# Attention on one core: softmax denominators from added key tiles, and a new order of masks, ropes, statistics, roots and denominators

## The reference

```python
q = (X @ Wq)...; k = (X @ Wk)...; v = (X @ Wv)...    # 16 query heads, 8 key/value heads, 32 wide
q = q * cos + _rotate_half(q) * sin                  # rope; k the same
k = jnp.repeat(k, n_rep, axis=1)                     # one key head serves two query heads
att = jnp.einsum('bhqd,bhkd->bhqk', q, k) * scale
att = SOFTCAP * jnp.tanh(att / SOFTCAP)              # cap at 50
att = jnp.where(causal[None, None], att, -jnp.inf)
att = jax.nn.softmax(att, axis=-1)
y = jnp.einsum('bhqk,bhkd->bhqd', att, v)
return y @ Wo
x = x + _L0_attn_ref(_layernorm(x, axis=-1), ...)
```

## Time and profile before

| | |
|---|---|
| median of 3 runs | 1013.99 us (1012.54 to 1015.94) |
| profiled execution | 1013.01 us, its span 1011.3 us, mean granted clock 0.977 |
| attention stage | about 346 to 684 us of the span, first scores at 365.7 us |
| busy over the whole span | PE 933.9 us (92%), DVE 654.7 (65%), ACT 537.3 (53%), POOL 484.2 (48%) |

### The profile page before, as it was taken

The page is one execution under the profiler, slowest core; times in us unless marked ns, Lnnn a source line. Parts: engine busy times, 40 slices in busy tenths (PEclk is TensorE's granted clock), DMA queues, the critical chain, the costliest instruction groups (busy, mean ns, idle before and its releaser), DMA issues. The chain is left out here.

```text
span 1011.3 us, 18264 instructions
## 1 busy us (share of the span) xinstructions
PE 933.9 (92%) x6274; PEld 695.2 (69%) x6274; DVE 654.7 (65%) x1670; ACT 537.3 (53%) x798; POOL 484.2 (48%) x534
## 2 busy tenths in 40 slices
PE   2999998999999589999999999868999989999998
PEld 1788885777778465666666666546888767777787
DVE  4888767544444456877877877646888676453435
ACT  3766642132233258888888888836667622232322
POOL 5333203555642067687687687524413124555540
PEclk9999999999999789999999999987999999999999
DMA  5434225777884300101101000103332256777735
GB/s 189 119 92 134 67 81 160 168 180 177 188 190 105 125 1 12 32 21 31 31 21 31 31 21 29 56 19 90 111 106 74 71 175 143 180 170 187 178 60 172
DMA packets 95432, 101.90 MB, mean 101 GB/s; under 512 B 18688, under 2 KB 86656, under 8 KB 95360
## 3 DMA queue, kind: packets, MB, share of 16 engines
q1 hardware_dynamic: 83072, 83.17, 27.6%
q0 software_dynamic: 12288, 17.83, 10.6%
HBM read 65.44 MB, written 35.54 MB: 100 GB/s over the span
## 5 line engine op out<-in xcount | busy, mean ns | idle before, releaser
L80 PE MATMUL gu<-x_hi,gu_hi 128*128 128x512 f32 x308 | 140.3, 455 | 4.7 <-DVE act_gu L1124 4.7
L82 PE MATMUL gu<-x_lo,gu_hi 128*128 128x512 f32 x308 | 122.8, 399 | 0.0
L81 PE MATMUL gu<-x_hi,gu_lo 128*128 128x512 f32 x308 | 122.4, 398 | 0.0
L1627 POOL TENSOR_SCALAR_AFFINE_SELECT probs_at<-probs_at 128x1024 f32<-128x1024 f32 x64 | 77.4, 1209 | 81.6 <-ACT probs_at L1551 80.9
L1543 ACT ACTIVATE capped_at<-scores_at 128x2048 f32<-128x2048 f32 x64 | 93.2, 1457 | 29.9 <-PE scores_at L1447 29.9
L671 POOL DMA_INDIRECT rows<-z_rows,slots x64 | 67.7, 1058 | 75.7 <-DVE slots L1115 56.7
L957 ACT CAST a_hi<-act_gu 128x512 fp32r<-128x512 f32 x96 | 59.2, 616 | 84.3 <-DVE act_gu L1124 66.9
L1551 ACT ACTIVATE probs_at<-capped_at 128x2048 f32<-128x2048 f32 x64 | 95.2, 1487 | 2.0
L80 PE MATMUL down<-down_hi,a_hi 128*128 128x256 f32 x300 | 93.8, 313 | 0.2 <-DVE a_lo L1134 0.2
L1005 ACT ACTIVATE y<-gu,rows 128x256 f32<-128x256 f32 x64 | 30.4, 474 | 109.8 <-PE gu L887 93.2
L867 PE MATMUL zT<-w_gu,xT 128*128 128x352 f32 x256 | 86.3, 460 | 0.0
(11 more groups left out here) (228 smaller groups left out, 2547.6 us busy)
## 6 DMA issues: line engine op xcount, KB each, us to landing
w_gu<-in_w_gate SPq DMA_DIRECT2D x64, 176.0 KB
w_gu<-in_w_up SPq DMA_DIRECT2D x64, 176.0 KB
w_down<-in_w_down SPq DMA_DIRECT2D x64, 176.0 KB
z_rows<-z SPq DMA_DIRECT2D x16, 512.0 KB, 3.1
acc<-base SPq DMA_DIRECT2D x10, 512.0 KB, 3.5
out<-base SPq DMA_DIRECT2D x10, 512.0 KB, 3.6
x_f<-in_X SPq DMA_DIRECT2D x8, 512.0 KB, 4.6
xn_at<-acc SPq DMA_DIRECT2D x16, 256.0 KB, 2.7
```

The costliest lines, as they stand in the source:

```text
L80: nc.tensor.matmul(out, w_hi, x_hi, start=first, stop=False)
L81: nc.tensor.matmul(out, w_lo, x_hi, start=False, stop=False)
L82: return nc.tensor.matmul(out, w_hi, x_lo, start=False, stop=last)
L1627: pool.affine_select(out=diag, in_=diag, compare_op=ALU.is_ge, fill=zero, base=0, pattern=[[0, JH], [0, REP], [1, P]], channel_multiplier= ...
```

## The change

The products with ones no longer run with the values of each unit. For the first 128 queries only key tile 0 counts; for the last 128 both tiles do. VectorE now adds the two tiles' probabilities for those last 128 queries (`add_tiles`, into a new buffer `both`), and a new TensorE step, `denominators`, makes eight products of 256 columns per group: four with ones and the first 128 queries of tile 0, four with ones and `both`. `probs` has one buffer for each of the four units, and `exponential` waits on the `denominators` of the slot before in place of the values of two units back. `invert` waits on `denominators`.

The lists change too. TensorE: `denominators`(b-1, 1) stands behind the first two pieces of the projection, `denominators`(b, 0) behind the output. ScalarE: `y_hi_part`(b, 0) moves from the end of the slot into the next slot, behind `take_values`(b, 1). GpSimd: root first, and the fourth mask ahead of the third rope. VectorE: `statistics` first, `y_lo`(b-1, 0) and `invert`(b-1, 1) behind the first two `turn`, `aT_lo_part` ahead of `divide`(b, 0), and the two `add_tiles`. Input buffers: 6 in place of 4. The waits at the end of the stage and ScalarE's loop (unrolled by 6 in place of 4) follow from that.

```diff
-        HELD = 4
+        HELD = 6
...
-        probs = sb("probs", [P, 2, JH, W], F32)
+        probs = sb("probs", [P, UNITS, JH, W], F32)
+        both = sb("both", [P, GROUPS, JH, REP, P], F32)
...
 (weighted_values, TensorE)
-                    at_least(pe, den_taken, b * GROUPS + g)
                 n = REP * (SEQ - t * P)
-                for bank, ones in ((den, True), (pv, False)):
+                for j in range(JH):
+                    w = v[:, q, t, (JH * g + j) * HD:(JH * g + j + 1) * HD]
+                    out = pv[j * HD:(j + 1) * HD, :].rearrange("p (r s) -> p r s", r=REP)[:, :, t * P:SEQ]
+                    last = nc.tensor.matmul(out, w, probs[:, u, j, 0:n].rearrange("p (r s) -> p r s", r=REP),
+                                            start=t == 0, stop=t == QT - 1)
+                last.then_inc(pv_done, 1)
+
+            def denominators(b, g):
+
+                pe.wait_ge(summed, b * GROUPS + g + 1)
+                at_least(pe, den_taken, b * GROUPS + g)
+                for of_both in (False, True):
                     for j in range(JH):
-                        w = m.ones_f[:] if ones else v[:, q, t, (JH * g + j) * HD:(JH * g + j + 1) * HD]
-                        out = bank[j * HD:(j + 1) * HD, :].rearrange("p (r s) -> p r s", r=REP)[:, :, t * P:SEQ]
-                        last = nc.tensor.matmul(out, w, probs[:, u % 2, j, 0:n].rearrange("p (r s) -> p r s", r=REP),
-                                                start=t == 0, stop=t == QT - 1)
-                last.then_inc(pv_done, 1)
+                        if of_both:
+                            weights = both[:, g, j]
+                        else:
+                            weights = probs[:, QT * g, j].rearrange("p (r s) -> p r s", r=REP)[:, :, 0:P]
+                        at = slice(of_both * P, (of_both + 1) * P)
+                        out = den[j * HD:(j + 1) * HD, :].rearrange("p (r s) -> p r s", r=REP)[:, :, at]
+                        last = nc.tensor.matmul(out, m.ones_f[:], weights, start=True, stop=True)
+                last.then_inc(den_done, 1)
...
 (slot_of, TensorE)
                     project(b + 1, 1 - q, 1)
+                if behind:
+                    denominators(b - 1, 1)
                 score_unit(b, q, 1)
...
                     output(b - 1)
+                denominators(b, 0)
                 weighted_values(b, q, 2)
...
 (exponential, ScalarE)
-                at_least(act, pv_done, b * UNITS + max(u - 1, 0))
+                at_least(act, den_done, (b - 1) * GROUPS + u // QT + 1)
...
 (slot_of, ScalarE)
                     take_values(b - 1, 1)
+                    y_hi_part(b - 1, 0)
...
-                y_hi_part(b, 0)
-                if further:
                     aT_hi_part(b + 2)
...
 (slot_of, GpSimd)
+                if further:
+                    root(b + 2)
                 causal(b, 0)
...
-                if further:
-                    root(b + 2)
                 causal(b, 2)
+                causal(b, 3)
                 if ahead:
                     rope(b + 1, 1 - q, 2)
-                causal(b, 3)
...
 (VectorE)
+            def add_tiles(b, g):
+
+                dve.wait_ge(probs_ready, b * UNITS + QT * (g + 1))
+                at_least(dve, den_done, (b - 1) * GROUPS + g + 1)
+                first = probs[:, QT * g].rearrange("p j (r s) -> p j r s", r=REP)[:, :, :, P:SEQ]
+                second = probs[:, QT * g + 1, :, 0:REP * P].rearrange("p j (r s) -> p j r s", r=REP)
+                dve.tensor_tensor(both[:, g], first, second, ALU.add).then_inc(summed, 1)
...
 (slot_of, VectorE)
-                if behind:
-                    y_lo_part(b - 1, 0)
-                    invert(b - 1, 1)
+                if further:
+                    statistics(b + 2)
                 if ahead:
                     turn(b + 1, 0)
                     turn(b + 1, 1)
                 if behind:
+                    y_lo_part(b - 1, 0)
+                    invert(b - 1, 1)
                     divide(b - 1, 1)
-                if further:
-                    statistics(b + 2)
                 if ahead:
                     turn(b + 1, 2)
                 if behind:
                     y_lo_part(b - 1, 1)
-                invert(b, 0)
+                add_tiles(b, 0)
                 if behind:
                     residual(b - 1)
-                divide(b, 0)
+                invert(b, 0)
                 if further:
                     aT_lo_part(b + 2)
+                divide(b, 0)
+                add_tiles(b, 1)
```

More of the change, by code:

```diff
@@ L1362, in attention @@
         pv_done = sem("pv_done")
+        summed = sem("summed")
+        den_done = sem("den_done")
         taken = sem("taken")
@@ L1394, in _ @@
                 if b == SEQS - 2:
-                    for n in range(HELD):
+                    for n in range(2 * BLK // SEQ):
                         sp.wait_ge(stored[n], 16)
@@ L1403, in _ @@
             for n in range(HELD):
-                sp.wait_ge(stored[n], 16 * (SEQS // HELD))
+                sp.wait_ge(stored[n], 16 * len(range(n, SEQS, HELD)))
         @block.tensor
@@ L1516, in _ @@
             weighted_values(SEQS - 1, 1, 3)
+            denominators(SEQS - 1, 1)
             output(SEQS - 1)
@@ L1548, in exponential @@
                 act.wait_ge(capped_ready, b * UNITS + u + 1)
-                at_least(act, pv_done, b * UNITS + max(u - 1, 0))
+                at_least(act, den_done, (b - 1) * GROUPS + u // QT + 1)
                 n = REP * (SEQ - u % QT * P)
-                nc.scalar.activation(probs[:, u % 2, :, 0:n], capped[:, u % 2, :, 0:n], ACT.Exp,
+                nc.scalar.activation(probs[:, u, :, 0:n], capped[:, u % 2, :, 0:n], ACT.Exp,
                                      scale=SOFTCAP).then_inc(exp_ready, 1)
@@ L1600, in _ @@
             take_values(SEQS - 1, 1)
+            y_hi_part(SEQS - 1, 0)
             y_hi_part(SEQS - 1, 1)
@@ L1625, in causal @@
                 n = REP * (SEQ - u % QT * P)
-                diag = probs[:, u % 2, :, 0:n].rearrange("p j (r s) -> p j r s", r=REP)[:, :, :, 0:P]
+                diag = probs[:, u, :, 0:n].rearrange("p j (r s) -> p j r s", r=REP)[:, :, :, 0:P]
                 pool.affine_select(out=diag, in_=diag, compare_op=ALU.is_ge, fill=zero, base=0,
@@ L1686, in turn @@
                 dve.stream_shuffle(turned[:, n], bank[:], [(i + HD // 2) % HD for i in range(HD)]).then_inc(turned_ready, 1)
+            def add_tiles(b, g):
[4 more added lines that the diff above has]
+                dve.tensor_tensor(both[:, g], first, second, ALU.add).then_inc(summed, 1)
             def invert(b, g):
                 n = b * GROUPS + g
-                dve.wait_ge(pv_done, b * UNITS + QT * (g + 1))
+                dve.wait_ge(den_done, n + 1)
                 dve.transpose(den_T[:].rearrange("p n d -> p (n d)"), den[:]).then_inc(den_taken, 1)
```

## The result

The changed kernel takes 1034.2 us (median of 6 runs, 1033.02 to 1035.26) against 1014.4 before: ratio 1.0195, 95% interval 1.0182 to 1.0209, so 2% slower. Its profiled execution spans 1033.5 us against 1011.3. The starts of the transposes and of the last residual divide the 22.2 us between them. Between the transposes of sequences 2 and 15 it is 266.7 in place of 248.3 (+18.4); from the first transposes to those of sequence 2, 29.6 in place of 30.5 (-0.9); from those of sequence 15 to the last residual, 53.1 in place of 48.7 (+4.4); all the rest is +0.3.

The account below looks back on a forecast made before the run. TensorE bound the kernel before; after the change the loop through VectorE and ScalarE would, at 20.7 us a slot. 13 periods (+20.5), slot 0 (-1.3) and the end (+1.7) gave 1033.9 profiled, 1034.5 forecast; range 1017 to 1046.

Parts of the forecast that it names:

- the ring: Attention slot: loop from one slot's transposes through VectorE and ScalarE to the next slot's, forecast to set a 20.7 us period.
- TensorE's gain: Attention slot: denominators at 0.46 us a set, 1.84 in place of 2.70, so TensorE's work falls 0.86 to 18.26 us.
- Steps 1 to 10: Attention slot: walk from transposes through VectorE, GpSimd and ScalarE to the next transposes, cap2 at 12.86, end at 20.70 us.
- The reading of how VectorE and GpSimd hold each other: Two-input VectorE operations and GpSimd's: whichever starts first finishes, the other runs afterwards; `divide` ended 0.55 us after GpSimd.
- `add_tiles` at 1.22: VectorE's 128x1024 add of two SBUF operands: forecast at its lower bound of 1.22 us, a sign of being right.
- the bound of 2.7: VectorE's `add_tiles`: upper bound of 2.7 us if it runs behind a 1.60 us GpSimd instruction.
- step 4: VectorE's statistics, moved to the slot's front: 1.18 us to the last instruction plus 0.17 for it, ready at 5.35.
- Step 6, the race: First group's `y_lo` on VectorE starts 0.11 us after GpSimd's rope multiply, waits it out and ends at 9.56.
- rival A: `y_lo` starts before GpSimd's rope multiply and takes 0.68 us: period 19.95, +11.2, 1024.5 us; chance 0.22.
- Rival C, the clock: TensorE's clock halves after its idle time ahead of the last scores in every slot: period 22.3, 1055 us; chance 0.08.
- The sum: Whole kernel: 13 periods x 1.58 = 20.5 us, slot 0 -1.3, the end +1.7, together +20.9.
- Rival B: TensorE stays the bound in the attention slots and the time falls by 10.8 to 1002.5 us; chance 0.08.

Follow-up runs that it names:

- e2: Changed kernel with the second group's add cut from 1024 columns to 2 for all sequences but the first: 1015.5 us.
- e4: Changed kernel with `y_lo` of the first group moved behind the second group's division: 1015.0 us.
- e3: Changed kernel with the first group's add cut from 1024 columns to 2 for all sequences but the first: 1034.6 us.
- e5: Changed kernel with the first group's `y_lo` behind the second division and the statistics computed one sequence further ahead: 1008.7 us.
- e1: Changed kernel with the statistics back behind the previous group's division and GpSimd's root behind the second rope: 1030.1 us.
- e10: Changed kernel with GpSimd's loop over pairs of slots written out, same instructions: 1035.2 us.
- e7: Changed kernel with sixteen more product instructions per slot on TensorE, in its idle time ahead of the last scores: 1028.2 us.

## Why the prediction was right

The forecast was 1034.5, the measurement 1034.2, and the mechanism is the one forecast: cutting a piece of the ring speeds the kernel up (e2, e4), cutting as much VectorE time beside it does not (e3). By the steps:

- *TensorE's gain.* The new products take 0.46 us a set as forecast (533.96 to 534.42 in the timeline), so the work went, and e5 shows what it is worth when TensorE is near to binding: 0.47 of the 0.86 us a slot.
- *Steps 1 to 10.* In the slot shown above cap2 starts at 13.06 after the transposes (forecast 12.86), the next transposes at 20.88 (20.70). The 0.20 us of idle time that only this slot has make up the difference; the others of its kind have cap2 at 12.5 to 12.8 and the next transposes at 20.4 to 20.6, a little under the forecast. The reading of how VectorE and GpSimd hold each other fits: `y_lo`, begun 0.05 after a 1.29 us multiply, ends 0.54 after it; the step had 0.55. The sign "`add_tiles` at 1.22" holds for the add on the ring (1.21). The other takes 2.3 us, within the bound of 2.7, and costs nothing where it stands.
- *A wrong reading.* The prediction says that operations with one operand, the statistics among them, show no stretch beside GpSimd. The trace before shows one: the last instruction of the statistics takes 1.12 us in most slots, against 0.17, here beside GpSimd's mask from 526.88 to 527.97. It did no harm to the forecast, since GpSimd waits when the statistics run in step 4, but it is what e1 met.

```profile
526.87 1.12 DVE L1673 TENSOR_SCALAR var_in_at<-moments_at 128x2 f32<-128x2 f32 x1
```

- *Step 6, the race, went both ways*, which neither the forecast nor rival A had: five periods in thirteen are rival A's, at 19.7 in the mean where that had 19.95. The forecast margin was 0.11 us, the measured one 0.05 to 0.07 in most slots where GpSimd was first (0.1 in e10), and GpSimd's loop takes it away in every second slot.
- *Rival C, the clock,* took part too, in three periods, with 1.1 to 1.3 us each in place of 1.8. The prediction gave it a chance of all slots or none, and named a clock that falls in the middle of slots as a sign of being wrong; to this extent it was.
- *The sum.* Five periods shorter than forecast (-1.0 us each), three longer (+1.1) and five about as forecast (-0.1) leave 18.4 where 20.5 was forecast. The start gave -0.9 for -1.3. The end gave +4.4 for +1.7: most of the rest is the clock, which stood at 0.50 from 684 to 688 us, so the output product of the last slot took 5.4 us (684.86 to 690.25) against some 3.1 before. In e7, whose clock held, the end gave +1.2. So the agreement to 0.3 us is partly luck: errors in the periods and at the end offset each other, and the profiled execution (1035.3) lies 1.1 above the median, where the forecast had set the median 0.6 above its own sum for that execution (1033.9).
- *Rival B* did not happen here. e5 comes nearest to it, with TensorE busy for 19.69 us in 20, and gains 5 to 6 us on the kernel before, about half of B's 10.8.

The run-to-run mix of the three kinds of period was seen in one profile per kernel only, so how it varies stays open.

## What to carry to other kernels

When work is moved from the busiest engine to another, follow one full ring of in-order lists from an event to its next occurrence and add up what stands on it. If the sum comes to the period, an engine's busy share does not tell what a piece of work costs: here 1.1 us of VectorE's time a slot were worth 18.7 us on the ring and nothing beside it. Whatever is needed late (here the low part of an operand, or statistics for a later sequence) belongs behind what is needed early on the same engine. When the engine just relieved begins to idle ahead of each burst of work, look at its granted clock.

## What was not expected of the hardware

An extra 1.0 us of products per slot made the kernel 6 us faster (e7), as the clock then stayed at 1.00 through the slots. And which of VectorE and GpSimd starts first, by 0.05 us or so, decides which of them is held: `y_lo` takes 0.67 or 1.78 us, GpSimd's multiply 1.81 or 1.29. Writing out GpSimd's loop (e10) was enough to change it. Even an add of 2 columns is held: it took 1.2 us in e3 and 0.15 in e2.
